# A graph network's last residual: stored negated in the output beforehand, and added to by GpSimd's final stores

## The reference, cut to what matters

```
    h = jnp.maximum(_layernorm(x, axis=-1), 0.0)
    x = x + _L0_gnn_ref(h, L0_gnn_W, L0_gnn_b, src, dst)
    h = jnp.maximum(_layernorm(x, axis=-1), 0.0)
    x = x + _L1_gnn_ref(h, edge_index, L1_gnn_W1, L1_gnn_att_src1, L1_gnn_att_dst1, L1_gnn_b1, L1_gnn_W2, L1_gnn_att_src2, L1_gnn_att_dst2, L1_gnn_b2)
    return x
```

## Time and profile before

| what | value |
|---|---|
| median of 3 runs | 5618.19 us (5616.4 to 5620.69) |
| the profiled execution | 5620.85 us, its span 5619.0 us |
| busy: PE, DVE, ACT, POOL | 82%, 71%, 38%, 74% of the span |
| tail, from VectorE's first instruction on own rows | 5558.8 to 5619.0 |
| mean rate of DMA | 111 GB/s |

### The profile page before, as it was taken

How to read it: one execution, slowest core, us unless ns; L and a number is a source line. 1 busy time by engine, 2 the same in 40 slices (tenths; PEclk the granted TensorE clock), 3 DMA queues, 4 the chain that set the end, 5 groups by cost and what they waited for, 6 DMA issues and landing times. The chain is left out here.

```text
span 5619.0 us, 90796 instructions
## 1 busy us (share of the span) xinstructions
PE 4589.0 (82%) x21089; PEld 2665.4 (47%) x21269; DVE 3991.6 (71%) x12181; ACT 2125.9 (38%) x7094; POOL 4145.2 (74%) x4277
## 2 busy tenths in 40 slices
PE   8888898888888888888888877777777777777773
PEld 7444444454444445444444455555544545555552
DVE  7666666666666665666666667877777777888778
ACT  4000000020000002000000078888888688888884
POOL 9677777777777777777777757777777477777775
PEclk7999999989999998999999879889898888999987
DMA  2443333333333333433333354444444344444445
GB/s 90 119 112 106 106 105 106 106 108 106 106 106 106 106 106 96 134 106 106 106 106 106 105 166 110 110 109 110 110 109 122 111 110 109 110 110 110 110 110 173
DMA packets 309626, 625.90 MB, mean 111 GB/s; under 512 B 85322, under 2 KB 180408, under 8 KB 309080
## 3 DMA queue, kind: packets, MB, share of 16 engines
q0 software_dynamic: 192928, 530.18, 33.7%
q1 hardware_dynamic: 109800, 88.52, 5.0%
q10 hardware_dynamic: 6384, 1.39, 0.2%
HBM read 573.24 MB, written 47.33 MB: 110 GB/s over the span
## 5 line engine op out<-in xcount | busy, mean ns | idle before, releaser
L708 POOL DMA_INDIRECT ring<-conv_tab,csrc x2346 | 2220.9, 947 | 748.2 <-PE main L1162 522.1
L1459 DVE TENSOR_TENSOR acc<-acc,main 128x264 f32 (+2 forms) x4160 | 1753.3, 421 | 872.7 <-PE main L1162 784.3
L1162 PE MATMUL main<-ring,oh 128*128 x4992 | 1719.4, 429 | 367.2 <-ACTq L870 278.9
L720 POOL DMA_INDIRECT ring<-attn_tab,sidx x1664 | 1601.0, 962 | 551.1 <-issue 377.3
L1162 PEld LDWEIGHTS main<-ring,oh 128*128 128x128 f32 x4992 | 823.0, 195 | 1348.1 <-issue 1258.6
L1151 PE MATMUL psad<-quiet 128*128 128x512 bf16 x4428 | 1336.6, 380 | 9.9 <-ACTq L870 0.4
L1269 PE MATMUL main<-ring,oh 128*128 128x264 f32 x3328 | 1136.1, 432 | 0.0
L1453 DVE TENSOR_SCALAR oh<-iota,dloc 128x128 f32<-128x128 f32 x2505 | 892.0, 356 | 164.5 <-DVE acc L1459 78.2
L995 ACT ACTIVATE ring<-ring 128x64 f32<-128x64 f32 x3328 | 908.3, 341 | 0.0
L1151 PEld LDWEIGHTS psad<-quiet 128*128 128x128 bf16 x4608 | 452.2, 98 | 335.8 <-issue 3.6
L1269 PEld LDWEIGHTS main<-ring,oh 128*128 128x128 f32 x3328 | 563.5, 213 | 21.8 <-issue 0.8
(11 more groups left out here) (221 smaller groups left out, 3669.4 us busy)
## 6 DMA issues: line engine op xcount, KB each, us to landing
ring<-conv_tab,csrc POOLq DMA_INDIRECT x2346, 2.7
ring<-attn_tab,sidx POOLq DMA_INDIRECT x1664
ring<-attn_tab SPq DMA_DIRECT2D x14, 896.0 KB, 9.3
conv_tab<-oh SPq DMA_DIRECT2D x12, 896.0 KB, 4.0
flag_room<-start_rows SPq DMA_DIRECT2D x416, 8.0 KB
flag_room<-end_rows SPq DMA_DIRECT2D x416, 8.0 KB
x_tab<-acc SPq DMA_DIRECT2D x7, 896.0 KB
oh<-x_tab SPq DMA_DIRECT2D x7, 896.0 KB
```

The lines of the kernel that those rows point to most:

```text
L708: pool.indirect_dma_start(ring3[:, c % U, 0:C], None, conv_tab[k], bass.IndirectOffsetOnAxis(ap=csrc[:, c:c + 1], axis=0)).then_inc(gather ...
L720: pool.indirect_dma_start(ring3[:, j, 0:TW], None, attn_tab[l], bass.IndirectOffsetOnAxis(ap=sidx[:, i * GB * G + j:i * GB * G + j + 1], a ...
L1162: nc.tensor.matmul(main[s % 4][:, 0:width], oh[:, (s % OHR) * P:(s % OHR + 1) * P], ring[:, bass.ds(slots[s % 8], width)], start=True, sto ...
L1459: nc.vector.tensor_tensor(a, a, main[k][:, 0:width], ALU.add).then_inc(added, 1)
```

## The change

The stored residual is turned round: GpSimd and VectorE now form bias - acc, which is x1 + bias with its sign turned against that of before. For blocks 0 to 5 SyncE stores it into the output tensor itself, where the final rows will stand; block 6 goes to a small buffer x1_last_tab. At the end VectorE handles the residual of block 6 alone (now an addition). Blocks 0 to 5 go out by DMAs with an accumulating store (accum_op), which add to what stands in the output. These are issued by GpSimd, behind its own 21 tiles; each waits for mid_ready of its block, which VectorE now raises after the product with rs. SyncE loads one residual block instead of seven, and waits at the end for the accumulating stores as well.

```
-                    sp.dma_start(rows_of(x1_tab, i, C), acc3[:, i * TB:(i + 1) * TB, 0:C]).then_inc(stored, 16)
+                    to = rows_of(out[0:(NI - 1) * TB * P, :], i, C) if i < NI - 1 else rows_of(x1_last_tab, 0, C)
+                    sp.dma_start(to, acc3[:, i * TB:(i + 1) * TB, 0:C]).then_inc(stored, 16)
...
-            x1_rows(0)
-            x1_rows(1)
             for q in range(4, NI):
                 rows_back(q)
-            x1_rows(2)
-            x1_rows(3)
-            for q in range(XB, NI):
-                store_result(q - XB)
-                x1_rows(q)
-            for q in range(NI - XB, NI - 1):
-                store_result(q)
+            x1_last_rows()
...
-            sp.wait_ge(stored, 16 * (2 * NI + 2))
+            sp.wait_ge(stored, 16 * (NI + 3))
+            sp.wait_ge(result_added, ADDED_FROM + 16 * (NI - 1))
...
-                nc.gpsimd.tensor_tensor(acc[:, t * AW:t * AW + C], acc[:, t * AW:t * AW + C], bias[:, :], ALU.subtract
+                nc.gpsimd.tensor_tensor(acc[:, t * AW:t * AW + C], bias[:, :], acc[:, t * AW:t * AW + C], ALU.subtract
...
+            for q in range(NI - 1):
+                pool.wait_ge(mid_ready, 2 * NT + TB * (q + 1))
+                nc.gpsimd.dma_start(rows_of(out[0:(NI - 1) * TB * P, :], q, C), acc3[:, q * TB:(q + 1) * TB, 0:C],
+                                    accum_op=ALU.add).then_inc(result_added, 16)
...
-                        if l < LAYERS - 1:
+                        if l < LAYERS - 1 or i < NI - 1:
                             last.then_inc(mid_ready, b - a)
                         else:
                             link(last)
                             if a == i * TB:
-                                dve.wait_ge(x1_back[i % XB], X1_FROM + 16 * (i // XB + 1))
-                            x1 = x1_in[:, i % XB, a - i * TB:b - i * TB, :]
-                            nc.vector.tensor_tensor(rows(a, b), rows(a, b), x1, ALU.subtract).then_inc(mid_ready, b - a)
+                                dve.wait_ge(x1_back, X1_FROM + 16)
+                            x1 = x1_in[:, a - i * TB:b - i * TB, :]
+                            nc.vector.tensor_tensor(rows(a, b), rows(a, b), x1, ALU.add).then_inc(mid_ready, b - a)
```

More of the change, by code:

```diff
@@ L65 @@
 LAST = 2
-XB = 4
 XE = 4
@@ L102, in gnn @@
         attn_tab = [dram(f"attn_tab{k}", (NT * P, TW)) for k in range(LAYERS)]
-        x1_tab = dram("x1_tab", (NT * P, C))
+        x1_last_tab = dram("x1_last_tab", (TB * P, C))
         ring = sb("ring", [P, RING * AW])
@@ L183, in gnn @@
         xa = acc[:, 0:NT * C].rearrange("p (t c) -> p t c", c=C)
-        x1_in = oh[:, 0:XB * TB * C].rearrange("p (b t c) -> p b t c", b=XB, c=C)
+        x1_in = oh[:, 0:TB * C].rearrange("p (t c) -> p t c", c=C)
         stat3 = stat[:, :].rearrange("p (t k) -> p t k", k=2)
@@ L350, in gnn @@
         FLAG_INCS = 16 * (2 * H + 3)
-        x1_back = flags_in
+        x1_back = flags_in[0]
+        result_added = gathered[GB]
+        ADDED_FROM = 16 * HOPS * len(range(GB, EC, U))
         X1_FROM = FLAG_INCS * LAYERS * (NG // GB)
@@ L592, in _, with x1_last_rows @@
                         rows_back(q)
[L594 to L607, removed]
+            def x1_last_rows():
+                groups_done = -(-TB * C // (G * P))
+                sp.wait_ge(products_done, CR + (HOPS + LAYERS) * S - (GB - groups_done) * G)
+                sp.dma_start(x1_in, x1_last_tab.rearrange("(t p) c -> p t c", p=P)).then_inc(x1_back, 16)
             for q in range(4):
@@ L1601, in bias_last_x1 @@
                 a = acc3[:, POOL_X1:NT, 0:C]
-                nc.vector.tensor_tensor(a, a, bias[:, :].rearrange("p (o c) -> p o c", o=1).to_broadcast([P, TB, C]),
+                nc.vector.tensor_tensor(a, bias[:, :].rearrange("p (o c) -> p o c", o=1).to_broadcast([P, TB, C]), a,
                                         ALU.subtract).then_inc(x1_last_biased, 1)
```

## The result

| | before | changed kernel |
|---|---|---|
| median of 9 runs | 5619.77 us | 5635.31 us |
| range | 5616.4 to 5623.36 us | 5631.44 to 5637.91 us |
| span of the profiled execution | 5619.0 us | 5633.4 us |
| ratio, 95% interval | | 1.0028 [1.0019, 1.0037] |

The change made the kernel slower by 0.28%, some 15.5 us. The prediction said 5636 us and slower by more than 0.2%.

A forecast was written before the change was run, and what follows sets the result against it. VectorE's chain bounds the tail before; after the change, the late accumulating stores: 5595.0 + 0.95 + 1.3 + 35.3 + 4.6 = 5637.2 us, 18.2 later than 5619.0; added to the median, 5636 us, range 5614 to 5662.

The forecast's parts named there:

- The place: Tail: all six accumulating stores, 5.5 MB, start at once behind GpSimd's 21st tile, at about 5595.0 us.
- VectorE's gain: Tail: six subtractions gone from VectorE save 14.1 us, less 1.4 and 0.6 given back, net 12.1 us.
- The wait at block 0: VectorE's addition of block 0 waits for GpSimd's tile until about 5562.0 instead of starting at 5561.45: 0.6 us.
- The alternation: Tail: one GpSimd tile per VectorE instruction, each tile starting about 0.4 us after one, VectorE paying 0.3 us.
- Issue and first row: GpSimd's stores: 0.95 us to issue one, bound 6.6; 1.3 us more to receipt beyond issue and rows.
- the issue-bound rivals: GpSimd's issue goes with rows, 6.6 us a store (5641 us) or 9.9 us (5661 us); chance 0.20.
- The price of a row: Accumulating stores: 46 + 59 = 105 ns per 1 KB row, 336 rows per engine, 35.3 us for six.
- rule of two source reads: Accumulating stores at half a copy's rate: 93 ns a row, six take 31.2 us, end at 5633.1 us.
- The full-rate rival: Accumulating stores: the second read hides, 46 ns a row, 15.5 us for six, 5616.6 us, no change; chance 0.22.
- One small term: End of the drain: 2.4 us more for the two engines that carry the 106-row store, 53 rows each.
- The rival on the other side: GpSimd's tiles run nearer 727 ns, free of VectorE's turns; stores start earlier, 5606 us; chance 0.04.

The follow-up runs named there:

- e3: Changed kernel with each accumulating store issued between GpSimd's tiles, block q behind the tiles of block q+1: ratio to before 0.9986, tail 52.65 us.
- e2: Changed kernel with the six stores plain and issued by SyncE as each block is ready, residual of blocks 0 to 5 left out: ratio to before 0.9978, tail 48.15 us.
- e4: Changed kernel with ScalarE weighing GpSimd's own tiles of blocks 1 to 6, GpSimd keeping block 0's three: ratio to before 0.9973, tail 44.5 us.
- e1: Changed kernel with GpSimd's six late stores plain instead of accumulating, residual of blocks 0 to 5 left out: ratio to before 1.0002, tail 61.3 us.
- e9: Changed kernel with six plain stores from SyncE, but the last store (106 rows) from GpSimd, residual of blocks 0 to 5 left out: one run, tail 49.8 us.
- e5: Kernel before with ScalarE instead of GpSimd weighing the own tiles of blocks 1 to 6, stores plain: ratio to before 0.9998, tail 54.6 us.

## Why the prediction was right, point by point

**The place.** The time was lost where it was expected: the six stores stand behind GpSimd's 21st tile, start together, and their drain ends long after VectorE. e3 moves them, with an empty instruction as the only other difference, and the 16 us of loss turn into 7.6 us of gain. This is shown.

**VectorE's gain.** 12.1 us forecast, 12.15 measured in the changed kernel (55.46 - 43.31) and 12.07 in e2's tail (60.22 - 48.15). The terms hold one by one. The wait at block 0 is 0.57 us (0.6 forecast). The profile puts it down to ScalarE, but ScalarE's eight instructions for that block (0.24 us each) were long done. It is GpSimd's third tile, as forecast: in e4, where GpSimd has these three tiles alone, they end at 5573.93 + 3.16 = 5577.09, and the addition starts at 5577.19. There is no wait at blocks 1 to 5, as GpSimd won a turn in the first. The instructions beside tiles take 2.25 to 2.32 us.

The alternation, one tile per VectorE instruction, holds: with three instructions a block instead of four, the 21 tiles took 36.0 us instead of 37.2, and the last one ended at 5593.1, within 0.3 us of the forecast counted from the tail's start.

**Issue and first row.** 0.95 us was taken and the bound was 6.6 us. The starts lie 0.98 us apart, and plain stores of the same 896 rows take 943 ns in e1, the same as a gather of 128 rows. The cost of an issue doesn't go with the rows, and the issue-bound rivals, with a chance of 0.2, fall. The Trainium skill ("DMA: Bandwidth & Descriptors", "Anatomy of one DMA — SWDGE (gpsimd) path") says that many descriptors cost little more; e1's 943 ns agree.

**The price of a row: the term that was off.** 105 ns was taken; steady, it is 82 ns, which makes 336 rows 27.6 us instead of 35.3, 7.7 us less. The error was to add a whole row of the software queue for the read of the destination. One part of it is the 59 ns, which came from gathers whose packets filled 33.7% of the engines' time; busy throughout in e1, that queue moves 1 KB in 51 ns (16 x 1.024 / 320). But even 46 + 51 is more than the 82 measured, so part of the second read hides behind the rest. The other line of the DMA view of 5618 to 5622 shows how:

```profile
q0 software_dynamic: 781, 0.79, 123.9%
```

The last number is the sum of the packets' durations as a share of the time of 16 engines, so one packet lasted 1.239 x 64 / 781 = 0.102 us. On the mean an engine had 1.24 of them under way, and so a row cost only 82 ns. The 59 ns were such a duration too, so the forecast added it up as if rows didn't overlap. That 105 comes so near to 102 may be chance; no run takes it apart.

The Trainium skill's rule of two source reads ("Collectives: The Full Stack", "The bandwidth ceiling: the fold count and why AG ≠ RS ≠ AR") gave an estimate of 93 ns. The trace lies below that too: 199 GB/s against 320 for the same stores without accumulation (e1) is 0.62, not half. The full-rate rival falls, and e1 is its measure: without the accumulation the tail is 61.3 us, about 1 us more than before.

**What was missing from the sum.** Two terms of the other sign hid most of the error. One is time in the drain beyond the steady price. It started slower than it went on: the changed kernel's DMA of 5596 to 5600 shows 97 ns a row.

```profile
DMA packets 662, 0.68 MB, mean 169 GB/s; under 512 B 0, under 2 KB 662, under 8 KB 662
```

These 662 rows, 41 for each engine at 15 ns more, make 0.6 us. The other is the end of the program, 3.4 us from the last byte instead of 0.6, which was not foreseen at all. In all: forecast tail 5637.2 - 5558.8 = 78.4 us, measured 76.25. Steady rows at 82 ns alone would have given 70.7. The last byte came at 72.8, 2.1 us later, of which the slow start is 0.6; the other 1.5 us no row separates. The last 3.4 us are the wait for GpSimd's DRAIN. One small term seems to hold: the last 2.6 us before the last byte go by at 31 GB/s and less (the row of the changed kernel under e9), about what two engines move at one row in 82 ns (12.5 GB/s each, an estimate), and the forecast had 2.4 us more for the two engines that carry the 106 rows. The forecast of 5636 was thus closer than its terms deserved: the place and the size of the loss were reasoned, the last few microseconds were luck.

**The rival on the other side**, GpSimd running free of VectorE's turns, did not happen by itself. In e4, which makes GpSimd free, the time goes the way that rival said and further: 44.5 us, 15.7 us below before. The rival asked for the full rate too, since all its six stores still started together, at 5585. e4 does without it, because its first store starts 7.1 us into the tail and each of the others with its block. Once the stores are spread over the tail, a block's accumulating store drains in about the time in which VectorE makes the next block, so the accumulating rate is enough.

## What to carry to other kernels

When work is moved from a busy engine to transfers, ask first where these transfers stand in the list of the engine that must issue them: here the saving of 12 us was real, and the same six stores cost 16 us behind the tiles, gained 7.6 us between them, and 15.7 us with the tiles given to ScalarE (5.7 of these are the tiles' own, e5). An accumulating store is worth its price of about 1.6 plain ones when it starts as its block gets ready and drains beside the work; queued at the end, six of them undid the whole gain. Sum the bytes that are still to go when the last engine finishes, and compare them with what the stage before spread out.

## What the runs showed of the hardware that was not expected

- An accumulating store moved one row of 1 KB a packet at 199 GB/s; the same store without accumulation moved 3.8 KB a packet at 320 GB/s (e1).
- The issue of a store of 896 rows held GpSimd for 0.94 to 1.08 us, like a gather of 128 rows, while its recorded duration was up to 5.2 us.
- GpSimd's DRAIN at the end of the program ended 3.2 to 3.3 us behind the last packet of its queue (seven runs, with and without accumulation), or 5.3 to 5.4 us behind its last tile where it had no transfer under way (four runs). Where that came last, the span went on for 3.4 to 4.4 us behind the last byte; it was 0.6 us in e1, where SyncE's transfer came last.
- The packets of the accumulating stores lasted 102 ns each and overlapped on the engines, one row in 82 ns; the sum of the durations was 123.9% of the engines' time.
- The 106-row store ran at some 41 GB/s from SyncE; from GpSimd it went at 226 to 282 GB/s (e9), and the tail was still 1.7 us longer than e2's, since GpSimd's DRAIN came last.
